# Two exact blocks of Q in place of one, gathered in Q's own bank, and Q's halves exchanged by DMA

## The chip, the cores and the metric

The kernel runs on one core of a Trainium2 chip. The metric is the device time of one execution in microseconds. A core has TensorE (PE, matmuls into PSUM), VectorE (DVE), ScalarE (ACT), GpSimd (POOL, which works on SBUF only) and SyncE (SP, which here only issues DMAs). Each engine works through its own instructions in order; semaphores tie them together.

## The reference

One decoder layer over x of shape (2, 512, 1024), in float32:

```
x = x + attn(layernorm(x))          # 32 heads of 128, 8 K/V heads, 4-bit codes with a scale per 128 rows
x = x + fake_quant(layernorm(x)) @ fake_quant(ctx)      # ctx: (2, 1024, 1024), 8-bit grids
x = x + layernorm(x) @ binarized(weight).T              # weight: (1024, 1024)

attn(h): q, k, v = h @ W_q, h @ W_k, h @ W_v
         W = (codes - 8) * scales                        # scales: one row per block of 128 input rows
         q, k = rope(q), rope(k)
         softmax(q k^T / sqrt(128) + causal mask) v, then @ W_o
```

What matters here is Q of one head and one batch element, 128 x 512 in transposed form: a sum over 8 blocks of 128 input rows, each block with its own scale per output column, followed by the rotary embedding (rope).

## The kernel before

**Precision by splitting.** Float32 products are made of float16 matmuls. Both operands are split into a high and a low half, and `three_products` (L737) adds high x high, high x low and low x high. A code less 8 is a small integer and exact in float16. So a block whose scale is applied after the product needs only two matmuls: the codes against the high and the low half of the input. K is made that way throughout. Of Q, one block in eight is (`q_exact`, L813), the other seven go by three products of scaled weights (`q_part`, L824).

**Slots.** After a prologue (layer norm, K, most of V, the first Qs) the attention runs in 64 slots `p`, one for each head and batch element, eight to a group `g`. A slot `p` works on several things at once, written out by hand in each engine's program:

- TensorE (`slot`, L949): three score blocks of `p` (`scores`), Q of `p + 2` (`q_part`, `q_exact`), four units of the output projection of an earlier head (`o_unit`, 4 matmuls each), and last the weighing of V by the probabilities of `p - 1` (`weigh`).
- DVE: maxima of the scores, the addition of every output unit into `x_acc` (`o_add`), scaling and low halves of the next Q weights (`piece_scale`, `piece_lo`), the low half of the attention output (`ao_rest`), Q's sum (`q_sum`), and `q_join`.
- ACT: exponentials, high halves of everything (`q_hi`, `piece`, `prob_split`, `ao_part`), conversion of the output codes (`o_cut`), `q_base` and `q_swap`.
- POOL: normalisation of the probabilities and their low halves, sine and cosine products of Q, Q's low half.
- SP: loads of codes and scales, and four DMA transposes of the probabilities a slot (`turn`).

In groups 1 to 4 (32 slots) ACT, DVE and POOL also quantise one half tile of ctx per slot; in slots 0 to 7 and 40 to 63 they also prepare a piece of the dense layer's weights, and SP transposes it.

**Q of slot p + 2, step by step** (for p + 2 >= 4). PSUM has one tile `side_ps` of two banks: `q_ps` for the running Q and `pv_ps` for the exact block and for the weighing.

1. TensorE: block 1 by three products into `q_ps` (L985), an output unit, the exact block 0 into `pv_ps` (L989), block 2, the third score block, an output unit, blocks 3 to 7 (L1002).
2. ACT, between the second and the third exponential: `q_base` (L1268) multiplies `pv_ps` by block 0's scale into `q_sum_in`, a tile in SBUF (`stage_o`).
3. DVE, after `piece_lo`: `q_join` (L2017) adds `q_ps` and `q_sum_in` into `q_sum_in`.
4. ACT, after `ao_part`: `swap` (L1187) copies the lower 64 partitions of `q_sum_in` to the upper 64 of `swapped`, and the reverse.
5. POOL, at the start of the next slot: `swapped` times sine, `q_sum_in` times cosine into `rot` (`q_turn`, L1650); DVE adds both.

`EXACT` (L59) is the number of columns of a Q piece that come straight from codes; a piece holds four blocks, and only pieces of even slots hold block 0.

## Time and profile before

| | us |
|---|---|
| median of 3 runs | 1080.07 (1079.74 to 1082.73) |
| the profiled execution | 1077.91 |
| its span | 1076.1 |
| TensorE busy | 1031.6 |
| VectorE busy | 939.9 |
| GpSimd busy | 784.4 |
| ScalarE busy | 726.4 |

The span runs from the first to the last recorded instruction of the execution; the time of the execution is 1.8 us longer. Busy times count overlapping matmuls once. The granted clock of TensorE is 1.00 of full speed (2.4 GHz) in nearly every stretch.

### The profile page before, as it was taken

What the parts mean: (1) busy time and instruction counts of PE and PEld (TensorE: products, weight loads), DVE (VectorE), ACT (ScalarE), POOL (GpSimd) and SP (SyncE); (2) the same over time, 40 slices, a digit from 0 to 9 for tenths busy, and PEclk for the clock granted to TensorE, in tenths of its full rate; (3) what the DMA queues carried; (4) which work ended last, traced back from release to release, by engine and by line L of the source; (5) the groups of instructions that cost most, each with busy time, mean ns of one, the idle gap of its engine ahead of it and who ended that gap; (6) DMA issues with size and microseconds to landing.
All of it is one profiled execution on the core that took longest, in us unless ns stands there. A gap on an engine that the chain in (4) does not pass through costs nothing.

```text
span 1076.1 us, 19064 instructions
## 1 busy us (share of the span) xinstructions
PE 1031.6 (96%) x5346; PEld 503.0 (47%) x5356; DVE 939.9 (87%) x1741; ACT 726.4 (68%) x1589; POOL 784.4 (73%) x849
## 2 busy tenths in 40 slices
PE   5999998999999999999999999999999998879998
PEld 3444443444454454445444545544454444444443
DVE  7988898799888888888988899999999999878863
ACT  5547757777887788788878886776777676463320
POOL 4678797888888788878878888989898988332100
PEclk9999999999999999999999999999999999999999
DMA  9683213678666666676667566777776765422543
GB/s 341 243 191 118 84 60 73 152 152 159 167 156 157 155 161 146 159 160 153 149 155 164 149 151 144 165 156 145 161 159 156 153 130 125 106 106 63 99 103 79
DMA packets 309827, 156.13 MB, mean 145 GB/s; under 512 B 257728, under 2 KB 270400, under 8 KB 309728
## 3 DMA queue, kind: packets, MB, share of 16 engines
q1 hardware_dynamic: 301952, 141.69, 56.7%
q10 hardware_dynamic: 7776, 13.37, 4.1%
q8 instruction: 31, 0.51, 0.2%
q14 instruction: 68, 0.56, 0.2%
HBM read 89.20 MB, written 4.19 MB: 87 GB/s over the span
## 4 chain that ended last, share of the span: by engine, by line
POOL 47%; PE 20%; issue 17%; DVE 12%; ACT 3%; DMA 1%; DVEq 0%; POOLq 0%; ACTq 0%; SPq 0%
POOL w_b L1646 14%; POOL prob L1639 13%; POOL swapped L1634 7%; PE proj_ps L1103 5%; POOL rot L1654 4%; POOL q_sb L1659 3%; DVE rot L2014 2%; POOL ctx_raw L1767 2%; PE proj_ps L1108 2%; PE score_ps L1074 2%; POOL w_b L1740 2%; PE out_ps L762 2%; PE score_ps L762 2%; DVE x_acc L2109 1%; PE proj_ps L741 1%
## 5 line engine op out<-in xcount | busy, mean ns | idle before, releaser
L1646 POOL TENSOR_TENSOR w_b<-prob,w_b 128x896 f16<-128x896 f32 (+2 forms) x192 | 188.3, 995 | 41.3 <-ACT w_b L1323 41.1
L1639 POOL TENSOR_SCALAR prob<-prob,row_inv 128x512 f32<-128x512 f32 (+3 forms) x256 | 166.1, 660 | 66.4 <-DVE row_inv L2187 60.6
L1296 ACT ACTIVATE prob<-score_ps,neg_max 128x512 f32<-128x512 f32 (+3 forms) x256 | 132.7, 522 | 74.5 <-DVE neg_max L2085 53.3
L741 PE MATMUL side_ps<-hT,w_a 128*128 128x512 f16 x444 | 168.3, 379 | 0.0
L739 PE MATMUL side_ps<-hT,w_a 128*128 128x512 f16 x444 | 168.3, 379 | 0.0
L740 PE MATMUL side_ps<-hT,w_a 128*128 128x512 f16 x444 | 168.3, 379 | 0.0
L2109 DVE SCALAR_TENSOR_TENSOR x_acc<-out_ps,o_now,x_acc 128x1024 f32<-128x1024 f32 x120 | 153.2, 1277 | 0.0
L2109 DVE SCALAR_TENSOR_TENSOR x_acc<-proj_ps,o_now,x_acc 128x1024 f32<-128x1024 f32 x120 | 152.7, 1273 | 0.0
L945 PE MATMUL proj_ps<-work,w_b 128*128 128x512 f16 x496 | 127.3, 379 | 4.5 <-issue 2.3
L945 PE MATMUL out_ps<-work,w_b 128*128 128x512 f16 x496 | 127.3, 379 | 0.9 <-DVE x_acc L2109 0.8
L2085 DVE CUSTOM_DVE_ANT_0 score_ps<-score_ps,mask_b 128x512 f32<-128x512 f32 (+3 forms) x256 | 121.9, 497 | 3.2 <-PE score_ps L908 3.1
L925 PE MATMUL side_ps<-work,v_sb 128*128 128x512 f16 (+3 forms) x768 | 114.8, 299 | 1.6 <-DMA work<-w_b 1.6
L1323 ACT ACTIVATE w_b<-prob 128x896 f16<-128x896 f32 (+2 forms) x192 | 99.4, 549 | 2.6 <-POOL prob L1639 0.9
L1634 POOL TENSOR_TENSOR swapped<-swapped,sin_t 128x512 f32<-128x512 f32 x77 | 99.7, 1295 | 1.1 <-ACT swapped L1190 1.1
L925 PEld LDWEIGHTS side_ps<-work,v_sb 128*128 128x128 f16 (+1 forms) x768 | 69.6, 98 | 46.4 <-DMA work<-w_b 2.6
L906 PE MATMUL score_ps<-k_sb,q_sb 128*128 (+4 forms) x256 | 77.0, 301 | 7.0 <-ACT prob L1296 5.0
L945 PEld LDWEIGHTS proj_ps<-work,w_b 128*128 128x128 f16 x496 | 47.3, 98 | 66.0 <-issue 9.7
L1659 POOL TENSOR_TENSOR q_sb<-rot,q_sb 128x512 f16<-128x512 f32 x62 | 72.1, 1163 | 6.4 <-ACT q_sb L1286 5.8
L907 PE MATMUL score_ps<-k_sb,q_sb 128*128 (+4 forms) x256 | 76.6, 299 | 0.0
L1654 POOL TENSOR_TENSOR rot<-stage_o,cos_t 128x512 f32<-128x512 f32 x60 | 76.2, 1269 | 0.0
L1278 ACT ACTIVATE stage_o<-side_ps,o_now 128x512 f32<-128x512 f32 x60 | 41.2, 687 | 48.4 <-issue 38.5
L908 PE MATMUL score_ps<-k_sb,q_sb 128*128 (+4 forms) x256 | 73.3, 299 | 0.0
(271 smaller groups left out, 2218.5 us busy)
## 6 DMA issues: line engine op xcount, KB each, us to landing
stage_c<-in_codes_dram SPq DMA_DIRECT2D x72, 256.0 KB, 2.8
stage_o<-in_codes_dram SPq DMA_DIRECT2D x64, 256.0 KB, 2.9
stage_s<-in_scales_dram SPq DMA_DIRECT2D x64, 256.0 KB, 3.5
ctx_raw<-in_ctx_dram ACTq DMA_DIRECT2D x32, 256.0 KB, 3.1
work<-w_b SPq DMA_TRANSPOSE x261, 3.1
x_acc<-in_x_dram SPq DMA_DIRECT2D x8, 512.0 KB, 8.4
k_sb<-in_codes_dram SPq DMA_DIRECT2D x16, 256.0 KB, 6.7
v_sb<-in_scales_dram SPq DMA_DIRECT2D x16, 256.0 KB, 7.1
```

Of the source, the lines that this page charges most:

```text
L739: pe.matmul(o, stat(0), mov(0), start=first, stop=False)
L740: pe.matmul(o, stat(0), mov(1), start=False, stop=False)
L741: return pe.matmul(o, stat(1), mov(0), start=False, stop=last)
L925: mm = pe.matmul(pv_ps[:, kb * P:S], v_sb[:, bass.ds(g, 1), l, b * TB + kb, :].rearrange("p a d -> p (a d)"), probT[:, m, at:kb + (TB - 1) ...
L945: mm = pe.matmul(o[:, b, :], o_codes[:, h % RING, cb * P:(cb + 1) * P], ao[:, h % 2, l, b * S:(b + 1) * S], start=l == 0, stop=l == 1)
L1296: ins = act.activation(prob[:, SCORE_AT[qb]:SCORE_AT[qb] + w], score_ps[:, score_bank(i, u), off:off + w], ACT.Exp, bias=neg_max[:, c:c + ...
L1634: pool.tensor_tensor(y, y, sin_t[:, :], ALU.mult).then_inc(done, 1)
L1639: return pool.tensor_scalar(prob[:, at:at + w], prob[:, at:at + w], row_inv[:, col:col + 1], P_UP, ALU.mult, ALU.mult)
L1646: ins = pool.tensor_tensor(prob16[:, 1, to:to + w], prob[:, at:at + w], prob16[:, 0, to:to + w], ALU.subtract)
L1654: pool.tensor_tensor(rot[:, :], q_sum_in, cos_t[:, :], ALU.mult).then_inc(q_cosed, 1)
L2085: ins = dve.tensor_tensor_reduce(s, s, mask_b[:, S - w:S], -1.0, MAX_FROM, ALU.add, ALU.min, neg_max[:, c:c + 1])
L2109: ins = dve.scalar_tensor_tensor(y, u, s, y, ALU.mult, ALU.add)
```

## The change

Blocks 0 and 1 of Q are both exact. Block 0's product goes to `q_ps`, block 1's to `pv_ps`, both early in the slot. ACT scales the first into `q_sum_in` (`q_base`, now ahead of the first exponential). DVE scales the second, adds `q_sum_in`, and writes the sum back into `q_ps` (`q_seed`, after the second maxima). TensorE then accumulates the remaining six blocks onto it without clearing the bank. ACT copies the finished Q to `q_sum_in` (`q_copy`, after the first split of the probabilities), and SP issues two DMAs that exchange its halves into `swapped` (`swap_q`), in place of ACT's two copies. POOL takes the cosine product in the same slot and only the sine product in the next.

The scale table gets one more column for block 1. The diff, without the table's sizes, the semaphores' names and a flag of `three_products`:

```diff
-EXACT = P
-EARLY = 2
+N_EXACT = 2
+EXACT = N_EXACT * P
...
+            def swap_q(p):
+                sp.wait_ge(q_copied, p - FIRST_PIECES + 1)
+                for a in (0, 64):
+                    sp.dma_start(swapped[a:a + 64, :], q_sum_in[64 - a:128 - a, :]).then_inc(q_swap_landed, 16)
...
+                    if by_parts(p + Q_AHEAD) and not (known(p) and p >= N_SLOTS - Q_AHEAD):
+                        swap_q(p + Q_AHEAD)
...
-                pe.wait_ge(ao_ready, p - 3)
-                for l in range(2):
-                    mm = pe.matmul(pv_ps, w_a[:, 0, h % RING * KB * P:(h % RING * KB + 1) * P],
-                                   hT[:, l, 0, i % B * S:(i % B + 1) * S], start=l == 0, stop=l == 1)
-                mm.then_inc(q_exact_done, 1)
+                for e, o in enumerate((q_ps, pv_ps)):
+                    if e == 0:
+                        if known(p) and p == FIRST_PIECES:
+                            pe.wait_ge(q_summed, 3)
+                        else:
+                            pe.wait_ge(q_copied, p - FIRST_PIECES)
+                    else:
+                        pe.wait_ge(ao_ready, p - 3)
+                    w = (h % RING * KB + e) * P
+                    for l in range(2):
+                        mm = pe.matmul(o, w_a[:, 0, w:w + P], hT[:, l, e, i % B * S:(i % B + 1) * S],
+                                       start=l == 0, stop=l == 1)
+                    mm.then_inc(q_exact_done[e], 1)
...
-                first = 1 if by_parts(p) else 0
+                first = N_EXACT if by_parts(p) else 0
...
-                    elif known(p) and p <= FIRST_PIECES:
-                        pe.wait_ge(q_summed, (1, 1, 3)[p - 2])
+                    elif known(p) and p < FIRST_PIECES:
+                        pe.wait_ge(q_summed, 1)
                     else:
-                        pe.wait_ge(q_joined, p - FIRST_PIECES)
+                        pe.wait_ge(q_seeded, p - FIRST_PIECES + 1)
                 for kb in kbs:
                     mm = three_products(q_bank(p), lambda l: w_a[:, l, (h % RING * KB + kb) * P:(h % RING * KB + kb + 1) * P],
-                                        lambda l: hT[:, l, kb, b * S:(b + 1) * S], kb == first, kb == KB - 1)
+                                        lambda l: hT[:, l, kb, b * S:(b + 1) * S],
+                                        kb == first and not by_parts(p), kb == KB - 1, by_parts(p))
...
-                    pe.wait_ge(q_based, p)
+                    pe.wait_ge(q_seeded, p)
...
                     o_unit(p - 1, prev[1], 3)
+                parts = by_parts(p + Q_AHEAD)
+                if has_ahead and parts:
+                    q_exact(*ahead)
                 scores(p, i, g, 1)
                 if v_at:
                     v_blocks(v_at[2], v_at[3])
-                parts = by_parts(p + Q_AHEAD)
-                if has_ahead and parts:
-                    q_part(*ahead, range(1, EARLY))
                 if has_o:
                     o_unit(p, i, 0)
-                if has_ahead and parts:
-                    q_exact(*ahead)
-                elif has_ahead:
+                if has_ahead and not parts:
                     q_part(*ahead, range(0, 1))
-                if has_ahead and parts:
-                    q_part(*ahead, range(EARLY, 3))
+                if has_o:
+                    o_unit(p, i, 1)
                 scores(p, i, g, 2)
                 if has_ahead and not parts:
                     q_part(*ahead, range(1, 3))
                 if v_at:
                     v_blocks(v_at[3], v_at[4])
-                if has_o:
-                    o_unit(p, i, 1)
                 if has_ahead:
-                    q_part(*ahead, range(3, KB))
+                    q_part(*ahead, range(N_EXACT if parts else 3, KB))
...
-                if by_parts(p):
-                    act.wait_ge(q_joined, p - FIRST_PIECES + 1)
-                swap(q_swap_of(p), q_sum_in if by_parts(p) else q_bank(p), q_swapped)
+                swap(q_swap_of(p), q_bank(p), q_swapped)
+            def q_copy(p):
+                act.wait_ge(q_done, p + 1)
+                act.activation(q_sum_in, q_bank(p), ACT.Copy).then_inc(q_copied, 1)
             def q_base(g, i):
                 p = g * SLOTS + i
-                act.wait_ge(q_exact_done, p - FIRST_PIECES + 1)
+                act.wait_ge(q_exact_done[0], p - FIRST_PIECES + 1)
                 if not (known(p) and p == FIRST_PIECES):
                     act.wait_ge(q_cosed, p)
+                    act.wait_ge(q_swap_landed, (p - FIRST_PIECES) * 32)
                 if known(p) and p < Q_LEAD * B:
                     act.wait_ge(o_table_ready, 2)
                 else:
                     act.wait_ge(o_now_ready, g * RF + (i // B - (Q_LEAD - 1)))
-                act.activation(q_sum_in, pv_ps, ACT.Copy, scale=o_now[:, (i // B + 1) % 2, CB:CB + 1])\
+                act.activation(q_sum_in, q_ps, ACT.Copy, scale=o_now[:, (i // B + 1) % 2, CB:CB + 1])\
                     .then_inc(q_based, 1)
...
+                if has_ahead and by_parts(p + Q_AHEAD):
+                    q_base(*((g, i + Q_AHEAD) if i < SLOTS - Q_AHEAD else (g + 1, i + Q_AHEAD - SLOTS)))
...
                 exps(p, i, 1)
-                if has_ahead and by_parts(p + Q_AHEAD):
-                    q_base(*((g, i + Q_AHEAD) if i < SLOTS - Q_AHEAD else (g + 1, i + Q_AHEAD - SLOTS)))
...
                 prob_split(p, 0)
+                if has_ahead and by_parts(p + Q_AHEAD):
+                    q_copy(p + Q_AHEAD)
+                elif has_ahead:
+                    q_swap(p + Q_AHEAD)
+                if has_prev and not (known(p) and p == N_SLOTS - 1):
+                    ao_part(p - 1, (i - 1) % SLOTS)
                 if with_ctx:
                     act.wait_ge(ctx_clipped, q + 1)
                     act.activation(ctx_raw[:, :], ctx_raw[:, :], ACT.Copy, bias=ROUND).then_inc(ctx_rounded, 1)
-                if has_prev and not (known(p) and p == N_SLOTS - 1):
-                    ao_part(p - 1, (i - 1) % SLOTS)
-                if has_ahead:
-                    q_swap(p + Q_AHEAD)
...
             def q_turn(p):
-                pool.wait_ge(q_joined, p - FIRST_PIECES + 1)
+                pool.wait_ge(q_copied, p - FIRST_PIECES + 1)
                 pool.wait_ge(q_ready, p)
                 pool.tensor_tensor(rot[:, :], q_sum_in, cos_t[:, :], ALU.mult).then_inc(q_cosed, 1)
...
-                        sine(swapped[:, :], q_swapped, p + 1, q_sined)
-                        q_turn(p + 1)
+                        pool.wait_ge(q_ready, p + 1)
+                        sine(swapped[:, :], q_swap_landed, (p + 1 - FIRST_PIECES) * 32 + 31, q_sined)
...
                     norm(1).then_inc(norm_done, 1)
+                    if by_parts(p + Q_AHEAD) and not (known(p) and p >= N_SLOTS - Q_AHEAD):
+                        q_turn(p + Q_AHEAD)
                     prob_rest(p, 0)
...
-            def q_join(p):
-                dve.wait_ge(q_done, p + 1)
+            def q_seed(g, i):
+                p = g * SLOTS + i
+                dve.wait_ge(q_exact_done[1], p - FIRST_PIECES + 1)
                 dve.wait_ge(q_based, p - FIRST_PIECES + 1)
-                dve.tensor_tensor(q_sum_in, q_bank(p), q_sum_in, ALU.add).then_inc(q_joined, 1)
+                if known(p) and p < Q_LEAD * B:
+                    dve.wait_ge(o_table_ready, 2)
+                else:
+                    dve.wait_ge(o_now_ready, g * RF + (i // B - (Q_LEAD - 1)))
+                dve.scalar_tensor_tensor(q_ps, pv_ps, o_now[:, (i // B + 1) % 2, CB + 1:CB + 2], q_sum_in, ALU.mult, ALU.add)\
+                    .then_inc(q_seeded, 1)
...
                 maxima(p, i, 1)
+                if has_ahead and by_parts(p + Q_AHEAD):
+                    q_seed(*((g, i + Q_AHEAD) if i < SLOTS - Q_AHEAD else (g + 1, i + Q_AHEAD - SLOTS)))
...
-                if has_ahead and by_parts(p + Q_AHEAD):
-                    q_join(p + Q_AHEAD)
```

On TensorE, one slot of the last groups, from the second score block to the second output unit. `side_ps<-hT,w_a` is Q, `x4` rows are output units. Before:

```order
L908 MATMUL score_ps<-k_sb,q_sb 128x128
L739 MATMUL side_ps<-hT,w_a 128x512
L740 MATMUL side_ps<-hT,w_a 128x512
L741 MATMUL side_ps<-hT,w_a 128x512
L945 MATMUL proj_ps<-work,w_b 128x512 x4
L820 MATMUL side_ps<-hT,w_a 128x512 x2
L739 MATMUL side_ps<-hT,w_a 128x512
L740 MATMUL side_ps<-hT,w_a 128x512
L741 MATMUL side_ps<-hT,w_a 128x512
L906 MATMUL score_ps<-k_sb,q_sb 128x256
L907 MATMUL score_ps<-k_sb,q_sb 128x256
L908 MATMUL score_ps<-k_sb,q_sb 128x256
```

The same place in the changed kernel, whose lines are numbered anew:

```order
L838 MATMUL side_ps<-hT,w_a 128x512 x4
L925 MATMUL score_ps<-k_sb,q_sb 128x384
L926 MATMUL score_ps<-k_sb,q_sb 128x384
L927 MATMUL score_ps<-k_sb,q_sb 128x384
L925 MATMUL score_ps<-k_sb,q_sb 128x128
L926 MATMUL score_ps<-k_sb,q_sb 128x128
L927 MATMUL score_ps<-k_sb,q_sb 128x128
L964 MATMUL proj_ps<-work,w_b 128x512 x4
L964 MATMUL out_ps<-work,w_b 128x512 x4
L925 MATMUL score_ps<-k_sb,q_sb 128x256
L926 MATMUL score_ps<-k_sb,q_sb 128x256
L927 MATMUL score_ps<-k_sb,q_sb 128x256
```

Both exact blocks (x4: two matmuls each) stand ahead of the second score block, a second output unit has moved ahead of the third, and all of the six blocks by three products come after it.

On ACT, a slot with ctx, from the first split of the probabilities (128x896) to the write of ctx (ISA and REGISTER_ALU rows are waits and their registers). Before:

```order
L1323 ACTIVATE w_b<-prob 128x896
L1409 ACTIVATE ctx_raw<-ctx_raw 128x512
L1331 REGISTER_ALU
L1332 ACTIVATE work<-side_ps 128x512
L1259 REGISTER_ALU
L1189 ACTIVATE swapped<-stage_o 64x512
L1190 ACTIVATE swapped<-stage_o 64x512
L1319 REGISTER_ALU
L1323 ACTIVATE w_b<-prob 128x128
L1323 ACTIVATE w_b<-prob 128x256
L1422 ISA
L1422 ACTIVATE k_sb<-ctx_raw 128x512
```

Changed, from the copy of Q on:

```order
L1284 ACTIVATE stage_o<-side_ps 128x512
L1350 REGISTER_ALU
L1351 ACTIVATE work<-side_ps 128x512
L1434 ACTIVATE ctx_raw<-ctx_raw 128x512
L1338 REGISTER_ALU
L1342 ACTIVATE w_b<-prob 128x128
L1342 ACTIVATE w_b<-prob 128x256
L1443 ISA
L1443 ACTIVATE k_sb<-ctx_raw 128x512
L1292 REGISTER_ALU
L1297 ACTIVATE stage_o<-side_ps,o_now 128x512
L1399 REGISTER_ALU
```

The copy (L1284) stands ahead of the attention output (L1351), the rounding of ctx (L1434) has moved behind it, the two half copies are gone, and `q_base` (L1297) comes at the slot's end, ahead of the next slot's first exponential.

## Rows read from the trace of the kernel before

**Rows 1.** The page's busy times: share of the span, number of instructions.
```profile
PE 1031.6 (96%) x5346; PEld 503.0 (47%) x5356; DVE 939.9 (87%) x1741; ACT 726.4 (68%) x1589; POOL 784.4 (73%) x849
```
**Rows 2.** Timeline of TensorE, one slot: start us, length us, engine, line, operation [idle before].
```profile
593.84 0.38 PE L906 MATMUL score_ps<-k_sb,q_sb 128*128 x1
...
598.69 0.10 PEld L906 LDWEIGHTS score_ps<-k_sb,q_sb 128*128 128x128 f16 x1 [0.43 <-ACT prob L1296]
...
599.90 0.38 PE L739 MATMUL side_ps<-hT,w_a 128*128 128x512 f16 x1
...
603.13 1.03 PE L945 MATMUL proj_ps<-work,w_b 128*128 128x512 f16 x4
```
**Rows 3.** Timeline of ScalarE in the same slot.
```profile
594.12 0.60 ACT L1332 ACTIVATE work<-side_ps 128x512 f16<-128x512 f32 x1 [0.28 <-PE side_ps L925]
...
594.74 0.63 ACT L1189 ACTIVATE swapped<-stage_o 64x512 f32<-64x512 f32 x1
...
596.03 0.61 ACT L1323 ACTIVATE w_b<-prob 128x128 f16<-128x128 f32 x2
...
596.56 0.61 ACT L1422 ACTIVATE k_sb<-ctx_raw 128x512 f32 x1
...
597.86 0.69 ACT L1296 ACTIVATE prob<-score_ps,neg_max 128x512 f32<-128x512 f32 x1 [0.69 <-ACT k_sb L1422]
...
598.44 0.20 ACT L1296 ACTIVATION_READ_ACCUMULATOR prob<-score_ps,neg_max 128x1 f32 x1
```
**Rows 4.** Timeline of VectorE: one slot, the next, and the start of a third.
```profile
594.75 0.69 DVE L2125 SCALAR_TENSOR_TENSOR work<-side_ps,work 128x512 f16<-128x512 f32 x1 [0.25 <-ACT work L1332]
...
597.88 1.28 DVE L2109 SCALAR_TENSOR_TENSOR x_acc<-proj_ps,o_now,x_acc 128x1024 f32<-128x1024 f32 x1
...
606.46 0.69 DVE L2125 SCALAR_TENSOR_TENSOR work<-side_ps,work 128x512 f16<-128x512 f32 x1 [0.24 <-ACT work L1332]
...
608.22 1.27 DVE L2109 SCALAR_TENSOR_TENSOR x_acc<-out_ps,o_now,x_acc 128x1024 f32<-128x1024 f32 x1
...
610.13 1.27 DVE L2109 SCALAR_TENSOR_TENSOR x_acc<-proj_ps,o_now,x_acc 128x1024 f32<-128x1024 f32 x1
...
618.24 0.69 DVE L2125 SCALAR_TENSOR_TENSOR work<-side_ps,work 128x512 f16<-128x512 f32 x1 [0.25 <-ACT work L1332]
```
**Rows 5.** Waits from 700 to 850 us: who for whom, us in total, times, longest.
```profile
POOL prob L1639 <- DVE row_inv L2187: 10.3, 13, 0.8
ACT swapped L1189 <- DVE stage_o L2021: 6.7, 13, 0.5
POOL w_b L1646 <- ACT w_b L1323: 6.5, 13, 0.5
DVE rot L2014 <- issue: 5.8, 13, 0.5
```
**Rows 6.** Timeline of VectorE: the same instruction, two slots apart, later.
```profile
831.64 0.67 DVE L2125 SCALAR_TENSOR_TENSOR work<-side_ps,work 128x512 f16<-128x512 f32 x1
...
855.28 0.68 DVE L2125 SCALAR_TENSOR_TENSOR work<-side_ps,work 128x512 f16<-128x512 f32 x1
```
**Rows 7.** Groups by line and shape, VectorE: count | busy us, mean ns | idle before.
```profile
L1860 DVE SCALAR_TENSOR_TENSOR w_a<-stage_s,w_a 128x512 f16<-128x512 f32 x34 | 33.6, 990 | 0.1
...
L1860 DVE SCALAR_TENSOR_TENSOR w_a<-stage_s,w_a 128x384 f16<-128x384 f32 x30 | 25.7, 858 | 0.4 <-ACT w_a L1184 0.4
...
L1878 DVE SCALAR_TENSOR_TENSOR x_acc<-score_ps,prob,x_acc 128x512 f32<-128x512 f32 x32 | 23.0, 744 | 4.8 <-PE score_ps L762 4.4
```
**Rows 8.** Timeline of a later slot's end: SyncE's load, the next slot's first matmul.
```profile
840.61 0.58 SPq L569 DMA_DIRECT2D stage_o<-in_codes_dram  x1
...
841.02 0.38 PE L906 MATMUL score_ps<-k_sb,q_sb 128*128 128x512 f16 x1
```
**Rows 9.** DMA issues from 550 to 700 us: count, KB each, median us to landing.
```profile
stage_o<-in_codes_dram SPq DMA_DIRECT2D x13, 256.0 KB, 2.6
...
w_b<-in_ffn_w_dram SPq DMA_DIRECT2D x4, 128.0 KB, 3.7
```

More of the change, by code:

```diff
@@ L234, in build @@
         stage_o = sb("stage_o", [P, 2, PIECE], I32)
-        o_now = sb("o_now", [P, 2, CB + 1], F32)
+        o_now = sb("o_now", [P, 2, CB + N_EXACT], F32)
         ident = sb("ident", [P, P], F32)
@@ L266, in build @@
         probT = work16[:, ao_w:ao_w + 2 * TURN_W].rearrange("p (l k t) -> p l k t", l=2, k=TURN_BLOCKS)
-        o_table = work16[:, ao_w + 2 * TURN_W:ao_w + 2 * TURN_W + 2 * NH * (CB + 1)].bitcast(F32).rearrange(
-            "p (h c) -> p h c", c=CB + 1)
+        o_table = work16[:, ao_w + 2 * TURN_W:ao_w + 2 * TURN_W + 2 * NH * (CB + N_EXACT)].bitcast(F32).rearrange(
+            "p (h c) -> p h c", c=CB + N_EXACT)
         q_scale_rows = stage_o[:, 1, 0:NH * KB].bitcast(F32)
@@ L439, in build @@
         q_done = sem("q_done")
-        q_exact_done = sem("q_exact_done")
+        q_exact_done = [sem(f"q_exact_done{e}") for e in range(N_EXACT)]
         q_based = sem("q_based")
-        q_joined = sem("q_joined")
+        q_seeded = sem("q_seeded")
+        q_copied = sem("q_copied")
         q_swapped = sem("q_swapped")
+        q_swap_landed = sem("q_swap_landed")
         q_cosed = sem("q_cosed")
@@ L736, in _, with three_products @@
         def _(pe):
-            def three_products(o, stat, mov, first, last):
-                pe.matmul(o, stat(0), mov(0), start=first, stop=False)
-                pe.matmul(o, stat(0), mov(1), start=False, stop=False)
-                return pe.matmul(o, stat(1), mov(0), start=False, stop=last)
+            def three_products(o, stat, mov, first, last, onto=False):
+                pe.matmul(o, stat(0), mov(0), start=first, stop=False, skip_group_check=onto)
+                pe.matmul(o, stat(0), mov(1), start=False, stop=False, skip_group_check=onto)
+                return pe.matmul(o, stat(1), mov(0), start=False, stop=last, skip_group_check=onto)
             def k_group(m, kb):
@@ L2035, in scale_table @@
                 rows = q_scale_rows.rearrange("p (h k) -> p h k", k=KB)
-                dve.tensor_scalar(o_table[:, 0:NH - Q_LEAD, CB], rows[:, Q_LEAD:NH, 0], Q_UP, None, ALU.mult)
-                dve.tensor_scalar(o_table[:, NH - Q_LEAD:NH, CB], rows[:, NH - Q_LEAD:NH, 0], Q_UP, None, ALU.mult)
-                dve.tensor_scalar(o_now[:, 1, CB:CB + 1], rows[:, Q_LEAD - 1:Q_LEAD, 0], Q_UP, None, ALU.mult)\
-                    .then_inc(o_table_ready, 1)
+                for e in range(N_EXACT):
+                    c = CB + e
+                    dve.tensor_scalar(o_table[:, 0:NH - Q_LEAD, c], rows[:, Q_LEAD:NH, e], Q_UP, None, ALU.mult)
+                    dve.tensor_scalar(o_table[:, NH - Q_LEAD:NH, c], rows[:, NH - Q_LEAD:NH, e], Q_UP, None, ALU.mult)
+                    ins = dve.tensor_scalar(o_now[:, 1, c:c + 1], rows[:, Q_LEAD - 1:Q_LEAD, e], Q_UP, None, ALU.mult)
+                ins.then_inc(o_table_ready, 1)
             def wf_difference(u):
```

## The prediction

> **What bounds the kernel now.** I read the page's busy shares first, then one slot engine by engine in order of time, then the waits of a later stretch and the queues. The profiled execution took 1077.91 us around a span of 1076.1 us, and TensorE is busy in 96% of it [rows 1]. That share needs care: the rows give a 512-column matmul 0.38 us, but 15 of them start in 3.23 us (599.90 to 603.13), one per 0.2153 us [rows 2]. The Trainium skill ("Trainium Kernel Development and Optimization", Performance Expectations) says matmul busy time misleads because matmuls are pipelined; the trace agrees with its 0.2153 against 0.38.
>
> A slot of the attention loop has 54 such units: 23 for Q (7 blocks of three products, one exact block of two), 16 for the output projection, 7.5 each for scores and weighing. 54 x 0.2153 = 11.63 us. Measured, from one `ao_rest` to the next but one: 594.75 to 618.24, so 11.74 a slot [rows 4], with the 0.1 us that the third score block waits for ACT's first exponential [rows 2, 3]. So in the 32 slots that also quantise the context, TensorE is the bound to within 0.1 us.
>
> In the 28 slots that prepare the dense weights (2 to 7 and 40 to 61) a slot is (855.28 - 831.64)/2 = 11.82 us [rows 6]. There a ring through four engines repeats its waits in every one of 13 slots: ACT's swap waits for DVE's join, POOL's subtraction for ACT, DVE's Q sum for POOL [rows 5]. That ring, not TensorE, holds the extra 0.19.
>
> **The change part by part.** I put time 0 at the slot's first score matmul, 593.84.
>
> TensorE: block 1 of Q goes from three products to two in 60 of the 64 head and batch pairs. One unit each: 60 x 0.2153 = 12.9 us, to 53 x 0.2153 = 11.41 a slot. Taken by its duration row it would be 60 x 0.38 = 22.8, which I reject for the reason above.
>
> DVE: the join goes, a tensor_tensor of the same 512 columns, and the seed comes; I set them equal. The trace has no seed with PSUM in and PSUM out. The nearest rows are the 0.69 of `ao_rest` (PSUM and SBUF in, SBUF out, [rows 4]) and the 0.744 of a scaled add from PSUM [rows 7]; I take 0.70, nearer the first, which also reads side_ps. The low half and the scaling of the exact 128 columns go in every other slot: 0.990 - 0.858 = 0.13 for 128 columns [rows 7], and about as much for the scaling, so 0.13 a slot on average. DVE gets shorter, but its seed now stands in front of TensorE's long Q run, while the join stood behind it.
>
> ACT: two half copies go (596.03 - 594.74 = 1.29) and one copy of 0.60 comes, in a place where ACT waited for the end of weighing anyway. But `q_base` moves in front of the first exponential. After weighing ends, ACT's queue is: attention output at 0.28 and 0.62 for it (to 594.74), rounding the same 0.62, last split 0.53, context write 0.61, DMA issue 0.69 (597.86 less 596.56 and that 0.61), `q_base` 0.62, then the exponential, 0.78 to its accumulator's end [rows 3]. Sum 4.75, against 598.64 - 593.84 = 4.80 before. TensorE wants the third score block after 22 units, 22 x 0.2153 = 4.74, a little earlier than before; with 0.05 for the signal (598.64 to 598.69, [rows 2]) it waits 0.06.
>
> The new handshake: weighing, ACT, DVE `ao_rest` at 0.91, maxima, `o_add`, maxima, seed, TensorE's Q run. In an even slot the seed starts 3.13 after `ao_rest` (594.75 to 597.88) and ends at 4.74, before TensorE arrives at 22 units and the third block, 5.07: no wait. In an odd slot DVE first copies `o_now`, so `o_add` ends at 0.91 + 1.76 + 1.27 = 3.94, and the output unit that was moved ahead of the third block, wanted at 18 units = 3.88, waits 0.11; the seed starts at 0.91 + 3.67 and ends at 5.28, where TensorE is at 5.17: 0.16 more [rows 4]. So 0.06 and 0.27, mean 0.16, and a slot of 11.41 + 0.16 = 11.57 instead of 11.74: 0.17 x 32 = 5.4 us.
>
> The weight slots: with join and swap gone, the ring is cut at two of its links. What is then late is DVE itself, 11.82 less its 0.45 of waiting (5.8 us in 13 slots, [rows 5]) less 0.13, so 11.24, and TensorE's 11.41. The handshake is the same there, with two engines near their limit; I take 0.05 for it, and 0.12 for the swap by DMA (below), 11.58 instead of 11.82: 0.24 x 28 = 6.7 us.
>
> POOL: the cosine moves from the slot's start to before the subtractions. POOL sits 10.3/13 = 0.8 us a slot before the normalisation [rows 5], so its sum is untouched; without that cover the 1.27 us of the cosine would stand before the low transposes.
>
> SP: two DMAs of 128 KB a slot, queued behind the load of output codes and in front of the four transposes. Every instruction behind `q_copied` on SP is a transpose that must wait for the end of weighing anyway. Cost nothing as long as SP's chain has room; in a weight slot the codes' load leaves only 0.41 us before the slot's end [rows 8], therefore the 0.12. The landing is the real unknown: `q_base` waits for the earlier swap to land and stands in front of the exponential. It must land by 3.35 of the next slot, the sum of what ACT does ahead of it (0.28 + 0.62 + 0.62 + 0.53 + 0.61 + 0.69). The trace has no SBUF to SBUF copy; its nearest rows are 2.6 us for 256 KB of codes and 3.7 for 128 KB of weights [rows 9]. Q's run ends at 5.17 + 18 x 0.2153 = 9.05, the copy then at 9.7 to 10.2 behind ACT's split, and the halves are issued at about 10.3 and 10.9; with 2.6 they land at 1.9 of the next slot, with 3.7 at 3.0. Both ends are hidden in context slots, and I take the middle, 2.5; what lies beyond them is rival A.
>
> The Trainium skill ("SBUF — State Buffer", Door 1) says that 64 partitions reach only half of the memory's DMA ports, which speaks against two halves of 64 rows; worked out as an estimate with its 2 us of fixed cost and 218 GB/s, a half lands after 2.6 us. No row here shows such a copy. By that page the sum stays as it is.
>
> The three extra table columns are prologue work beside a TensorE that has its own queue; I charge 0.5 us for them and for the first two changed slots. Sum: 5.4 + 6.7 - 0.5 = 11.6 us. From the profiled 1077.91 that gives 1066.3; the median of the runs, 1080.07, is 2.2 above that execution, within what single executions differ, and I stay at 1066.
>
> **The rivals.**
> A, the swap lands late (slower). The chance for it is in the queue: in weight slots SP before issued the output codes at 0.41 before the slot's end, so the second half would be issued at 0.7 of the next slot (two issues of the codes' 0.58 behind it) and land, with 3.7, at 4.4. Then `q_base`, exponential and third score block are late by 4.4 + 0.62 + 0.78 + 0.05 - 4.74 = 1.1 us, and the slot is 12.5: 28 x 0.7 = 20 us lost, while the context slots break even. Half of that, because SP's weight transposes are released earlier by a DVE that no longer waits: about 1088. It decides from a landing at 3.6: above it the wait (3.6 + 1.45 - 4.74 = 0.31) eats what 11.74 - 11.41 would give. Against it: in context slots SP is idle between its loads.
> B, no change: the handshake costs 0.3 a slot and not 0.16, because DVE, with 11.41 - 11.24 = 0.17 us a slot to spare in weight slots, reaches `ao_rest` late as it does in weight slots now. Then 11.71 everywhere: 0.03 x 32 + 0.11 x 28 = 4 us less, or nothing if it is 0.4: 1074 to 1079. For it speaks that `o_now`'s copy stands in the chain, against it that DVE has an idle wait for ACT before `ao_rest` in context slots.
> C, more than forecast: no seed wait at all and the ring gone, 11.45 in context slots (9.3 us) and 11.41 in weight slots (11.5 us): 1057.
> That the change does not do what it says I set aside: one matmul in 54 is gone from the queue by count.
>
> **How the numbers follow.** Forecast (1060 to 1073) 0.58, A 0.15, B 0.14, C 0.13. No change is within 0.3%, 3.2 us, about what a measurement of this kernel tells: 1077 to 1083. Faster: 0.58 + 0.13 + a third of B = 0.76. Same: two thirds of B less a little, 0.08; slower: A and its neighbours, 0.16. Range: from C's 1057 to 1082, which leaves out most of A and a little below C.
>
> **What would show it.** Matmuls of Q: 60 fewer. Slots of about 11.55 in both kinds, odd ones longer by 0.2. TensorE's waits: the second output unit for `x_acc`, the first Q product for the seed, only in odd slots. ACT without a wait in front of `q_base` in context slots, and a wait there for a DMA if A holds. The waits of the ring (swap for join) gone, DVE's wait before the Q sum gone. The forecast is wrong if context slots are above 11.7 or if the exponential starts later than 4.1 us into its slot.

## The result, and the profile after

The changed kernel takes 1097.54 us (median of 4 runs, 1094.4 to 1099.28), the kernel before 1080.28 beside it: a ratio of 1.016, 95% interval 1.0145 to 1.018. It is slower by 17 us; 1066 was forecast, with a range that ended at 1082. The profiled execution took 1094.4 us around a span of 1092.6. All ratios below leave out one execution of 2784.25 us, one of the four of a kernel called e_hyb; all others lie within 1% of their kernel's median.

The page's busy times, to be read against [rows 1]:

```profile
PE 1029.3 (94%) x5296; PEld 495.0 (45%) x5296; DVE 972.6 (89%) x1744; ACT 684.7 (63%) x1529; POOL 776.2 (71%) x849
```

The 60 weight loads fewer and the 42 us less of ACT are as the change says. DVE is the odd one: it was to get shorter and is busy 33 us longer. Its timeline in an odd context slot shows where, with POOL's beside it (start us, length us, engine, line, operation, idle before):

```profile
616.35 1.27 POOL L1675 TENSOR_TENSOR rot<-stage_o,cos_t 128x512 f32<-128x512 f32 x1
617.40 0.69 DVE L2156 SCALAR_TENSOR_TENSOR work<-side_ps,work 128x512 f16<-128x512 f32 x1 [0.98 <-ACT work L1351]
617.57 1.89 POOL L1667 TENSOR_TENSOR w_b<-prob,w_b 128x896 f16<-128x896 f32 x1
618.01 1.48 DVE L2126 COPY o_now<-work 128x10 f32 x1
619.41 0.69 DVE L2116 CUSTOM_DVE_ANT_0 score_ps<-score_ps,mask_b 128x512 f32<-128x512 f32 x1
620.02 1.27 DVE L2140 SCALAR_TENSOR_TENSOR x_acc<-out_ps,o_now,x_acc 128x1024 f32<-128x1024 f32 x1
...
621.34 0.55 PEld L964 LDWEIGHTS out_ps<-work,w_b 128*128 128x128 f16 x4 [1.21 <-DVE x_acc L2140]
621.35 0.82 PE L964 MATMUL out_ps<-work,w_b 128*128 128x512 f16 x3 [0.72 <-DVE x_acc L2140]
```

The copy of ten floats a row into `o_now` takes 1.48 us. It ends at 619.49; POOL's subtraction of 896 columns, which was running when it began, ends at 617.57 + 1.89 = 619.46. What the copy takes too long is handed on: the maxima, `o_add` (621.29), TensorE's output unit. The kernel before had the same pair, in the slot of [rows 4]:

```profile
605.77 1.89 POOL L1646 TENSOR_TENSOR w_b<-prob,w_b 128x896 f16<-128x896 f32 x1
606.46 0.69 DVE L2125 SCALAR_TENSOR_TENSOR work<-side_ps,work 128x512 f16<-128x512 f32 x1 [0.24 <-ACT work L1332]
607.07 0.63 DVE L2095 COPY o_now<-work 128x9 f32 x1
```

Again the copy (to 607.70) ends just after the subtraction (607.66). But there the subtraction had begun 1.30 us before the copy, now 0.44: the moved cosine stands in front of it. In weight slots the subtraction used to be over when the copy came (794.66 + 1.88 = 796.54, copy at 796.66), and the copy took 0.16:

```profile
794.66 1.88 POOL L1646 TENSOR_TENSOR w_b<-prob,w_b 128x896 f16<-128x896 f32 x1
...
796.66 0.16 DVE L2095 COPY o_now<-work 128x9 f32<-128x9 f32 x1
```

The groups by line and shape give all copies of the kernel after (first row the loop's context slots, second mostly the weight slots; busy us, mean ns):

```profile
L2126 DVE COPY o_now<-work 128x10 f32 x16 | 22.1, 1381 | 0.0
...
L2126 DVE COPY o_now<-work 128x10 f32<-128x10 f32 x16 | 17.5, 1092 | 0.0
```

Before they were 633 and 289 ns, so the sum is 24.9 us more. In the kernel before, 19 of the 32 copies took longer than 0.16 us, in the kernel after 31. The Trainium skill ("SBUF — State Buffer", SBUF: two separate sides) says that DVE and GpSimd share one pair of ports as a lock held for a whole instruction, and that a two-port DVE operation which meets a running GpSimd operation blocks until its end. These rows agree, with 0.03 us between the two ends; that the copy is a two-port operation, no row shows.

The waits of the whole span (who for whom, total us, times, longest):

```profile
POOL prob L1660 <- DVE row_inv L2220: 127.0, 62, 3.4
...
ACT stage_o L1297 <- DMA swapped<-stage_o: 60.1, 29, 3.7
...
PEld out_ps L964 <- DVE x_acc L2140: 33.1, 38, 1.6
...
PE out_ps L964 <- DVE x_acc L2140: 17.1, 28, 1.1
PEld score_ps L925 <- ACT prob L1315: 16.7, 22, 1.4
```

The other large part of DVE's 33 us is the low half of the Q weights: 78.4 us for its two shapes, 59.3 before (last section).

Two suspects stand here: the output unit behind the late `o_add`, and `q_base`, which waits 60 us for the swap's DMA. The ring's waits of [rows 5] are gone, as forecast.

As a table, the mean distance from one `ao_rest` to the next: the six weight slots before the loop, the 32 of the loop (its turns' longer first slots included, in all kernels), and 18 of the later weight slots. The last columns are the medians of the two alternating distances.

| kernel | us | first 6 | context 32 | weights 18 | context, odd / even | weights, odd / even |
|---|---|---|---|---|---|---|
| before | 1080 | 11.74 | 11.87 | 11.86 | 11.78 / 11.70 | 11.95 / 11.68 |
| after | 1098 | 12.35 | 12.17 | 12.04 | 12.81 / 11.38 | 12.48 / 11.45 |

Every other context slot takes 11.38, the forecast TensorE bound of 11.41 to within 0.03. The one with the copy is 1.0 longer than in the kernel before.

### The profile page after: what moved, and what is told of

It reads as the page before. It is cut to its first block, busy times and chain, and to the rows that moved or that the text cites. A ratio compares the mean times of both kernels' runs of the same rounds, so it can differ in the third digit from the quotient of the medians.

```text
span 1092.6 us, 19144 instructions
## 1 busy us (share of the span) xinstructions
PE 1029.3 (94%) x5296; PEld 495.0 (45%) x5296; DVE 972.6 (89%) x1744; ACT 684.7 (63%) x1529; POOL 776.2 (71%) x849
## 4 chain that ended last, share of the span: by engine, by line
PE 59%; DVE 16%; SPq 9%; issue 6%; ACT 4%; POOL 3%; DMA 2%; DVEq 0%; ACTq 0%; POOLq 0%
PE side_ps L944 7%; PE side_ps L749 6%; PE side_ps L750 6%; PE side_ps L751 6%; PE proj_ps L964 5%; PE out_ps L964 5%; PE proj_ps L1118 4%; SPq L664 4%; DVE x_acc L2140 3%; DVE o_now L2126 3%; PE proj_ps L1123 2%; DVE score_ps L2116 2%; PE score_ps L1089 2%; SPq L679 2%; PE side_ps L838 2%
## 5 line engine op out<-in xcount | busy, mean ns | idle before, releaser
L1660 POOL TENSOR_SCALAR prob<-prob,row_inv 128x512 f32<-128x512 f32 (+3 forms) x256 | 162.4, 646 | 132.7 <-DVE row_inv L2220 127.0
L1667 POOL TENSOR_TENSOR w_b<-prob,w_b 128x896 f16<-128x896 f32 (+2 forms) x192 | 185.9, 997 | 0.9 <-ACT w_b L1342 0.7
L749 PE MATMUL side_ps<-hT,w_a 128*128 128x512 f16 x384 | 145.4, 379 | 2.9
L751 PE MATMUL side_ps<-hT,w_a 128*128 128x512 f16 x384 | 145.5, 379 | 0.0
L750 PE MATMUL side_ps<-hT,w_a 128*128 128x512 f16 x384 | 145.5, 379 | 0.0
L1297 ACT ACTIVATE stage_o<-side_ps,o_now 128x512 f32<-128x512 f32 x60 | 41.1, 685 | 69.6 <-DMA swapped<-stage_o 60.1
L925 PE MATMUL score_ps<-k_sb,q_sb 128*128 (+4 forms) x256 | 77.0, 301 | 7.5 <-ACT prob L1315 7.1
L964 PEld LDWEIGHTS out_ps<-work,w_b 128*128 128x128 f16 x496 | 46.0, 98 | 84.0 <-DVE x_acc L2140 33.1
L1351 ACT ACTIVATE work<-side_ps 128x512 f16<-128x512 f32 x64 | 38.2, 597 | 69.4 <-PE side_ps L944 69.3
L2156 DVE SCALAR_TENSOR_TENSOR work<-side_ps,work 128x512 f16<-128x512 f32 x64 | 44.0, 688 | 39.2 <-ACT work L1351 33.8
L1883 DVE SCALAR_TENSOR_TENSOR w_a<-stage_s,w_a 128x256 f16<-128x256 f32 (+1 forms) x64 | 78.4, 1225 | 0.5 <-ACT w_a L1199 0.4
```

The source lines that it names most:

```text
L749: pe.matmul(o, stat(0), mov(0), start=first, stop=False, skip_group_check=onto)
L750: pe.matmul(o, stat(0), mov(1), start=False, stop=False, skip_group_check=onto)
L751: return pe.matmul(o, stat(1), mov(0), start=False, stop=last, skip_group_check=onto)
L964: mm = pe.matmul(o[:, b, :], o_codes[:, h % RING, cb * P:(cb + 1) * P], ao[:, h % 2, l, b * S:(b + 1) * S], start=l == 0, stop=l == 1)
L1660: return pool.tensor_scalar(prob[:, at:at + w], prob[:, at:at + w], row_inv[:, col:col + 1], P_UP, ALU.mult, ALU.mult)
L1667: ins = pool.tensor_tensor(prob16[:, 1, to:to + w], prob[:, at:at + w], prob16[:, 0, to:to + w], ALU.subtract)
```

## The experiments

Each ran beside the kernel before on its chip (1078.8 to 1079.8 there).

**e_gap: the copy moved.** DVE makes it an even slot earlier, behind the Q sum:

```diff
 (odd slot)
-                    j = o_scales(g, i)
+                    j = g * RF + i // B
 (even slot, behind q_sum(p + 1))
+                if i % B == 0 and not (known(p) and p + 1 < O_LAG):
+                    o_scales(g, i)
```

> The changed kernel with one DVE instruction moved: the copy of the ten scales into o_now stands at the end of the even slots, behind the Q sum, where POOL is idle, and no longer between ao_rest and o_add of the odd slots, where a POOL subtraction of 1.89 us is running. Lock theory (the copy waits out POOL's running instruction, and the moved cosine shifted the subtractions onto it): the copy takes 0.16 to 0.3 us, the odd slots fall from 12.7 to about 11.5, the time is 1062 to 1074. Column theory (ten float32 a row are slow to copy, nine are not): the copy still takes over 1.1 us wherever it stands, 1085 to 1100. Late-swap theory (the halves of Q land late and hold q_base and the exponential): the time falls by less than 10.

1074.32 us, ratio 0.9957 (0.9942 to 0.9972): by the ratios 22 us less than the changed kernel, and 0.3 above the range expected. The copies, from 560 to 660 us (min, median, max ns):

```profile
L2126 DVE COPY o_now<-work x4: 163/166/167, 573.8 to 642.5; 128x10 f32 x3, 128x10 f32<-128x10 f32 x1
```

Context slots are 11.62 (11.55 / 11.38). But the weight slots hardly moved: 12.02, and 12.43 for the first six. The lock theory holds for the context slots, and a second cost was behind it in the others.

**e_act: the copy given to ScalarE.**

```diff
 (ScalarE, behind exps(p, i, 0) of the odd slots)
+                    act.activation(o_now[:, of[1] % 2, :], <row of o_table>, ACT.Copy).then_inc(o_now_ready, 1)
```

> The changed kernel with the copy into o_now done by ScalarE, behind the first exponential of the odd slots; DVE does not do it any more. Lock theory: ScalarE does not share what DVE and POOL share, so the copy takes about 0.2 to 0.3 us in every slot whatever POOL does, and the time is 1062 to 1076 (ScalarE's 0.3 us in half of the slots is hidden). Column theory: if the width is slow for every engine, ScalarE's copy takes over 1 us. Late-swap theory: less than 10 us gained.

1073.75 us, ratio 0.9943 (0.9925 to 0.996). The copy takes 199 and 207 ns on the average, whatever POOL does:

```profile
L1408 ACT ACTIVATE o_now<-work 128x10 f32 x16 | 3.2, 199 | 0.0
L1408 ACT ACTIVATE o_now<-work 128x10 f32<-128x10 f32 x15 | 3.1, 207 | 0.0
```

Context 11.62, weights 12.16: the same picture on another engine.

**b_ten: ten columns in the kernel before.**

```diff
-        o_now = sb("o_now", [P, 2, CB + 1], F32)
+        o_now = sb("o_now", [P, 2, CB + 2], F32)
```

> The kernel before with a table of ten columns in place of nine, and so o_now copied at 128x10; nothing else is changed, the tenth column is filled and not read. Lock theory: the copy keeps its two durations (about 0.63 us in the loop's slots, where a subtraction of POOL ends 0.6 us after its start, and about 0.2 to 0.3 in the weight slots), the time is that of the kernel before within 3 us. Column theory: the copy takes 1.1 us or more and the kernel loses 20 us or more.

1078.76 us, ratio 1.0003 (0.9993 to 1.0013), the copies 648 and 287 ns. The column theory has fallen.

```profile
L2096 DVE COPY o_now<-work 128x10 f32 x16 | 10.4, 648 | 0.0
L2096 DVE COPY o_now<-work 128x10 f32<-128x10 f32 x16 | 4.6, 287 | 0.0
```

**e_cos: the cosine moved back by one subtraction.**

```diff
-                        q_turn(p + Q_AHEAD)
                     prob_rest(p, 0)
                     ...
+                        q_turn(p + Q_AHEAD)
                     prob_rest(p, 1)
```

> The changed kernel with the cosine moved again on POOL: behind the 896-column subtraction and in front of the two small ones. Lock theory: the 1.89 us subtraction runs 1.27 us earlier and ends about 0.2 us after the o_now copy starts in context slots, so that copy falls from 1.4 to 0.3 to 0.5 us (or stays near 1.3 where the cosine gets hold first), and the time is 1074 to 1090 with the copy where it was. Column theory: no change of the copy. Cost on the other side: the small subtractions and their transposes come 1.27 us later.

1089.38 us, ratio 1.0111 (1.0091 to 1.0131), 6 us less than the changed kernel by the ratios. DVE's copy and POOL in one context slot:

```profile
609.53 1.88 POOL L1667 TENSOR_TENSOR w_b<-prob,w_b 128x896 f16<-128x896 f32 x1
611.38 1.27 POOL L1675 TENSOR_TENSOR rot<-stage_o,cos_t 128x512 f32<-128x512 f32 x1
```
```profile
610.85 0.60 DVE L2126 COPY o_now<-work 128x10 f32 x1
```

The copy ends at 611.45, behind the subtraction's 611.41. With nothing changed but POOL's order, the mean of the loop's copies went from 1381 to 414 ns, of the others only from 1092 to 1032: in the later weight slots the copy now meets the cosine (1.27 us) and ends 0.02 to 0.04 us behind that. Context slots fell to 11.94, not to 11.62: `q_base` now waits 42.8 us for the cosine. So the order on POOL sets how long the copy takes, and a cosine one subtraction later is no cure. The cosine's old place, in the next slot, was not run in the changed kernel.

**b_gap: the copy moved in the kernel before.** The edit of e_gap on the kernel before.

> The kernel before with the o_now copy moved into the even slots' gap. Lock theory: the copy falls from 0.63 to 0.17 us in the context slots and stays 0.16 in the weight slots; since TensorE (11.63) and the ring bind there, the time moves by 0 to 5 us only, 1074 to 1080: the place of the copy matters only beside the moved cosine.

1077.87 us, ratio 0.9989 (0.9978 to 0.9999), with the loop's copies at 0.17 us. The copy's wait was nearly free there, about 1 us in all; the collision became dear only in the changed kernel.

**e_actswap and e_actswap_gap: no DMA.** The halves by two ScalarE copies behind `ao_part`, in all slots, without and with e_gap's edit:

```diff
-                        swap_q(p + Q_AHEAD)
+                if has_ahead and by_parts(p + Q_AHEAD):
+                    q_swap(p + Q_AHEAD)
```

> The changed kernel with the halves of Q exchanged by ScalarE again (two half copies of 0.65 us behind ao_part), not by DMA; the seed, the moved cosine and the copy of o_now stay. Lock theory: the copy of o_now still takes 1.1 to 1.5 us, the odd slots stay at 12.5 or more, and the first exponential comes up to 1.3 us later in all slots, so the time is that of the changed kernel or more, 1095 to 1125. Late-swap theory: without the wait for the landing (60 us at q_base) the kernel is faster than the changed one by 10 us or more.

> The changed kernel with both: o_now copy in the gap, and the halves of Q exchanged by ScalarE in all slots. Queue theory: weight slots 11.45 as in the hybrid; context slots are late at the exponential, since ScalarE has 1.29 us more in front of it than its 4.7, so 12.0 in even and odd ones: 1068 to 1082. If a landing that comes late were the cost in context slots too, these would be 11.5 or less and the time under 1062.

1103.35 us, ratio 1.022 (1.0203 to 1.0237), and 1083.56, ratio 1.0056 (1.0038 to 1.0074; 1.6 above what was expected). With before and after they complete a table:

| swap, place of the copy | context | weights 18 | us |
|---|---|---|---|
| DMA, in the chain (after) | 12.17 | 12.04 | 1098 |
| DMA, in the gap (e_gap) | 11.62 | 12.02 | 1074 |
| ScalarE, in the chain | 12.59 | 11.90 | 1103 |
| ScalarE, in the gap | 12.31 | 11.52 | 1084 |

In context slots the DMA swap is worth 0.4 to 0.7 a slot. In weight slots it costs 0.5 with the copy in the gap (12.02 - 11.52) and 0.14 with it in the chain, and the copy's 0.38 is only seen once the DMA is gone: the two hide each other.

**b_dma: the DMA swap alone, in the kernel before.** `swap_q` on SP waits for the join, and ScalarE's half copies go:

```diff
+                sp.wait_ge(q_joined, p - FIRST_PIECES + 1)
+                for a in (0, 64):
+                    sp.dma_start(swapped[a:a + 64, :], q_sum_in[64 - a:128 - a, :]).then_inc(q_swap_landed, 16)
```

> The kernel before with one part of the change: the halves of Q exchanged by DMA in place of ScalarE (join, subtractions, cosine and copy of o_now as before). Queue theory: SP's sum in a weight slot goes from 10.8 to 11.9, so these slots go from 11.82 to about 12.0 (5 us lost), while the context slots, bound by TensorE's 11.63, gain 0 to 0.1 each: 1077 to 1087. Prediction's view (the swap's DMA is hidden, ring relieved): 1071 to 1078.

1078.68 us, ratio 0.9998 (0.9989 to 1.0008). The prediction's view was 0.7 us off at its upper end, the queue theory's range held. The zero is a sum of two: context slots 11.65 (0.22 less), weight slots 12.06 (0.20 more), the first six 12.32 (0.58 more).

**b_hyb: the same, in the context slots only.**

```diff
-                    if by_parts(p + Q_AHEAD) and not (known(p) and p >= N_SLOTS - Q_AHEAD):
+                    if with_ctx and by_parts(p + Q_AHEAD) and not (known(p) and p >= N_SLOTS - Q_AHEAD):
                         swap_q(p + Q_AHEAD)
```

> The kernel before with the halves exchanged by DMA in the 32 context slots only, by ScalarE as before in the weight slots. From the run with the DMA in all slots: context slots 11.65 in place of 11.87, weight slots 11.82 as before: 32 x 0.22 = 7 us less than before, 1070 to 1075. If the gain of the context slots came from something that the weight slots lose (traffic moved, not saved), no change.

1073.55 us, ratio 0.9945 (0.9929 to 0.9962), as expected.

**e_hyb: the change with both costs removed.** The copy as in e_gap, SP's swap as in b_hyb; in slots without context ScalarE behind `ao_part`:

```diff
+                act.activation(swapped[0:64, :], q_sum_in[64:128, :], ACT.Copy).then_inc(q_swap_landed, 16)
+                act.activation(swapped[64:128, :], q_sum_in[0:64, :], ACT.Copy).then_inc(q_swap_landed, 16)
```

> The changed kernel with the o_now copy in the even slots' gap, and the halves of Q exchanged by two ScalarE copies in the slots without context (2 to 7 and 40 to 61) and by DMA only in the 32 context slots. Queue theory (in weight slots SP's own instructions, 4 transposes of Q's attention weights 5.8 us, 2 weight transposes 2.4, three loads 2.1 to 2.6, and the two swaps 1.1, sum to 11.9 and bind the slot): the weight slots fall from 12.0 to 11.45, 28 x 0.55 = 15 us less than with the moved copy alone, 1056 to 1063. If it is not SP's queue but TensorE, DVE or POOL that holds the weight slots at 12.0: no change, 1070 to 1076.

1063.09 us, ratio 0.9842 (0.9823 to 0.9862): by the ratio 17 us below the kernel before, at the upper edge of what was expected. First six 11.53, context 11.70, weights 11.51. TensorE makes up 77% of the chain that ended last; in the changed kernel it was 59%, in the kernel before 20%, with POOL at 47%:

```profile
PE 77%; DVE 8%; ACT 4%; issue 4%; DMA 3%; POOL 2%; SPq 1%; ACTq 0%; DVEq 0%; POOLq 0%
```

**What in the DMA costs: three runs.** In a weight slot of e_gap, SP's timeline shows no gap, so that SP's own time looks like the bound:

```profile
824.99 1.24 SPq L679 DMA_TRANSPOSE v_sb<-w_b  x1
826.27 0.58 SPq L571 DMA_DIRECT2D stage_o<-in_codes_dram  x1
826.89 1.11 SPq L653 DMA_DIRECT2D swapped<-stage_o  x2
828.11 5.77 SPq L664 DMA_TRANSPOSE work<-w_b  x4
```

ScalarE's of the same slot shows the late landing:

```profile
825.84 0.58 ACT L1284 ACTIVATE stage_o<-side_ps 128x512 f32<-128x512 f32 x1
827.24 0.60 ACT L1351 ACTIVATE work<-side_ps 128x512 f16<-128x512 f32 x1 [0.82 <-PE side_ps L944]
...
831.15 0.69 ACT L1297 ACTIVATE stage_o<-side_ps,o_now 128x512 f32<-128x512 f32 x1 [2.81 <-DMA swapped<-stage_o]
```

And TensorE's where it arrives, at the third score block:

```profile
832.56 0.28 PE L925 MATMUL score_ps<-k_sb,q_sb 128*128 128x256 f16 x1 [0.60 <-ACT prob L1315]
```

e_spload is e_hyb with SP's two issues left in the weight slots and nobody waiting for them; e_actq and e_actq2 are e_hyb with the DMAs of the weight slots issued by ScalarE, behind `ao_part` and behind `q_copy`:

```diff
 (e_spload, SP)
+                            sp.dma_start(dead[a:a + 64, :], cos_t[64 - a:128 - a, 0:48])
 (e_actq, e_actq2, ScalarE)
+                    act.dma_start(swapped[a:a + 64, :], q_sum_in[64 - a:128 - a, :]).then_inc(q_swap_landed, 16)
```

> The hybrid kernel (ScalarE copies the halves in the weight slots) with SP still issuing two DMAs of 64 partitions there, in the place of the swap's: 192 bytes a partition of a table into a tile that nothing reads and nobody waits for. It adds SP's instructions alone, no wait for a landing. Queue theory (SP's own sum, 11.9 us, binds the weight slots): they go from 11.5 to 11.9 or 12.0, 1072 to 1076. Landing theory (only the wait of q_base for the late halves costs): they stay at 11.5 to 11.6, 1062 to 1066.

> The hybrid kernel with one difference: in the weight slots too the halves of Q go by DMA, but ScalarE's queue issues the two DMAs (behind ao_part), not SP's. The bytes and the landing stay as in the changed kernel, only SP's 1.1 us a slot are gone. Queue theory (SP's own instructions bound the weight slots): they are 11.5 as in the hybrid, 1060 to 1067. Landing theory (the transfer itself, 2.6 to 3 us, and its traffic among the transposes held the weight slots at 12.0): they stay near 12.0 and the time is 1071 or more.

> The hybrid kernel with the halves of Q in the weight slots by DMA from ScalarE's queue, now issued right behind the copy of Q and ahead of ao_part (in the run before they stood behind ao_part, 1.3 us after the copy's end, and landed 4.2 us after ao_part's start; the slots took 12.9). Landing theory (a weight slot is as long as the landing makes it, whoever issues): landing about 3.0 after ao_part's start, so q_base comes at its old place and the slots fall to 11.5 to 11.7, 1062 to 1068. If the DMA itself is what costs (its traffic between the transposes), the slots stay at 12 or more, 1071 and more.

| kernel | us | ratio (95%) | first 6 | weights 18 |
|---|---|---|---|---|
| e_spload | 1063.25 | 0.9847 (0.9826 to 0.9868) | 11.54 | 11.60 |
| e_actq | 1102.39 | 1.0221 (1.0191 to 1.0252) | 12.76 | 12.87 |
| e_actq2 | 1065.88 | 0.9876 (0.9855 to 0.9898) | 11.57 | 11.61 |

The queue theory, on which I had built the expectations of e_hyb, e_actswap_gap, b_dma and e_actq, has fallen: SP's own sum does not bound the slot. SP in e_spload has as many instructions as in e_gap, and the slot is 11.60 in the mean all the same:

```profile
826.84 1.24 SPq L682 DMA_TRANSPOSE v_sb<-w_b  x1
828.13 0.59 SPq L574 DMA_DIRECT2D stage_o<-in_codes_dram  x1
828.76 1.11 SPq L713 DMA_DIRECT2D dead<-cos_t  x2
829.98 5.22 SPq L667 DMA_TRANSPOSE work<-w_b  x4
```

The row of four transposes takes 5.22 us here and 5.77 there, while the median of a single one from 660 to 865 us is the same, 1.24 and 1.25 us (the longest 1.28 and 1.77). So the row of e_gap, from its first start to its last end, holds waiting that it doesn't show. (The dead DMAs carry 192 bytes a row and not 2048, so this run leaves the bytes out; e_actq2 has them in.) What orders the runs is the landing, from `ao_part`'s start to `q_base`'s: 831.15 - 827.24 = 3.91 in e_gap (mean slot 12.02). In e_actq and e_actq2, the example slots:

```profile
804.68 0.60 ACT L1357 ACTIVATE work<-side_ps 128x512 f16<-128x512 f32 x1 [1.25 <-PE side_ps L944]
804.69 1.13 ACTq L1285 DMA_DIRECT2D swapped<-stage_o  x2
...
808.92 0.69 ACT L1303 ACTIVATE stage_o<-side_ps,o_now 128x512 f32<-128x512 f32 x1 [2.44 <-DMA swapped<-stage_o]
```
```profile
817.48 1.12 ACTq L1285 DMA_DIRECT2D swapped<-stage_o  x2
818.70 0.60 ACT L1357 ACTIVATE work<-side_ps 128x512 f16<-128x512 f32 x1 [1.25 <-PE side_ps L944]
...
821.82 0.69 ACT L1303 ACTIVATE stage_o<-side_ps,o_now 128x512 f32<-128x512 f32 x1 [2.02 <-DMA swapped<-stage_o]
```

4.24 (mean slot 12.87) and 3.12 (11.61). Averaged over the 18 weight slots the distance is 3.59 us in e_gap, 4.54 in e_actq and 2.92 in e_actq2, the same order. The same DMAs with the same bytes, issued 1.2 us earlier against `ao_part`, give 1.26 us a slot back. e_actq missed its expectation because I had put its issue behind an instruction that waits for the end of weighing.

SP's queue has a part in it all the same, by when it issues and not by its sum. In e_gap's slot the copy of Q ends at 825.84 + 0.58 = 826.42, but SP, still at its weight transpose and the codes' load, issues the first half at 826.89. From the copy's end to the first issue there are 0.03 us on average in e_gap's 32 context slots and 0.68 (up to 1.74) in its 18 weight slots, in e_actq2's 0.03. That is about what `q_base` gains there, 3.59 - 2.92 = 0.67. So a full SP costs nothing where nobody waits for the landing (e_spload), and the DMA little where it is issued at once (e_actq2); together they make the slot of 12.02.

## Why the prediction was wrong

*The `o_now` copy taken as 0.54 in odd context slots (the seed starts 3.67 behind `ao_rest` in place of 3.13) and given no price of its own in weight slots, so that `o_add` ends at 3.94.* This is the step that failed. It was read as a property of the copy, while the 0.63 in the trace was already a wait for POOL. In the slot shown `o_add` ends at 621.29, 4.71 after the first score matmul at 616.58, and the output unit, forecast to wait 0.11, waits 0.72 (its weights 1.21). With the copy out of the way the context slots are 11.55 / 11.38, in the mean 11.46, where 11.57 was forecast; with it, 12.81 / 11.38. Its price there is (12.17 - 11.62) x 32 = 18 us. With it fell "DVE gets shorter": DVE is busy 33 us longer, not less.

*POOL: the cosine moves, its sum is untouched.* True in the main (784.4 us before, 776.2 after) and the wrong question. POOL had time for the move, but what counted was which of its instructions runs while DVE copies.

*The swap's landing, 2.5 us, and 0.12 a weight slot for it.* The landing was nearly right in context slots (2.4 from 550 to 700 us) and too short in weight slots, where the issue also comes later behind SP's queue; the tile's view, from 740 to 860 us in the kernel after:

```profile
  ACT stage_o L1297: 22.6, 10
...
DMA to landing us min/median/max: 2.9/3.1/3.7
```

Rival A named this mechanism, the queue included, with its place and a deadline of 3.35 us into the slot. In e_gap's slot the halves are there at 831.11 - 827.04 = 4.1; by A's formula 4.1 + 1.45 - 4.74 = 0.8 us that the third score block is late. It starts at 832.56 - 827.04 = 5.52, so 0.78 behind 4.74 (the row's 0.60 of idle time counts from the modelled end of the matmul before). A's 12.5 us a slot was too much, 12.0 is measured; but the 0.12 was too little: 12.02 - 11.51, and 12.43 - 11.53 in the first six, make about 15 us over 24 slots (e_hyb itself is only 11 us faster than e_gap: its context slots came out at 11.70, not 11.62, and the four weight slots behind the 18 are 0.4 longer). A alone would not have made the kernel slower than before: e_gap, which still has it, is at 1074, where A said 1088.

*The two do not add in weight slots*: removing the copy's wait alone gave nothing there, removing the DMA alone 0.14, both 0.53. Between the profiled executions of the changed kernel and e_hyb (1094.4 and 1063.48 us, so 31 apart) lie (12.17 - 11.70) x 32 = 15 us in context slots, the copy's, and 14.5 in the 24 weight slots of the table, copy and landing together.

*What held.* A TensorE unit less is 0.2153 us: slots of 11.38 are 53 units' 11.41 to 0.03. The seed was 752 ns against 0.70. The ring of waits was gone; ACT's order with `q_base` ahead of the exponential costs nothing when the halves are there. e_hyb, with the block removed and neither cost, is 17 us faster than before. The count gives 12.9 of it to TensorE's units; the rest, the ring by the forecast, was not measured apart. The forecast of 11.6 us was a fair estimate of this kernel, not of the one that was changed, and in part by luck, since this one has no DMA swap in its weight slots. The lock was not among the rivals, though the row that shows it stood beside rows that I used.

What stays open: why the transfer itself, from issue to landing, is longer in weight slots. ScalarE's issues there land as late after the issue (median 3.4 in e_actq2, 2.3 in its context slots), so it isn't the issuing queue. The other transfers of these slots are the likely reason, not separated here; in b_dma, whose swaps are issued up to 1.6 us behind `ao_part`, the median there is 2.7.

## What to carry to other kernels

Before moving an instruction on GpSimd, lay its timeline over VectorE's: a small copy between SBUF tiles on the critical chain that takes several times its shortest duration may be waiting for a GpSimd instruction, as here, and its price is the phase between the two, which a busy-time sum doesn't show. Move such a copy to where GpSimd is idle, or give it to ScalarE. A DMA in place of engine copies has a deadline of its own in each kind of slot, and the queue that issues it may be busy when its data are ready; take it only in those that meet it, and where a part of a change measures as nothing, look for a gain and a loss in different stretches.
